# Fused attention and mixture-of-experts on one core: the gate's transposes move ahead of the score projection, its logits move beside the output projection

## What is computed

```python
def _layernorm(x, axis=-1, eps=1e-05): ...
# attention, 8 sequences of 1024 tokens, width 256, the heads not split
qkv = jnp.einsum('bse,he->bsh', x, w_qkv)
q, k, v = jnp.split(qkv, 3, axis=-1)
scores = jnp.einsum('bqh,bkh->bqk', q, k) * scale
out = jnp.einsum('bqk,bkh->bqh', jax.nn.softmax(scores, axis=-1), v)
out = jnp.swapaxes(out, 1, 2).reshape(Bn, Sn, H)
out = jnp.einsum('bsh,eh->bse', out, w_proj) + b_proj
# expert layer: 16 experts, each takes its 1024 best tokens
logits = flat_x @ gate_w.T
scores = jax.nn.softmax(logits, axis=-1).T
topk_weight, topk_idx = jax.lax.top_k(scores, C)
g, u = xg @ Wg.T, xg @ Wu.T                # per expert
h = jax.nn.gelu(g, approximate=False) * u  # then Wd, weighted, scatter-added
# plus a shared expert of the same shape over all tokens
x = x + _layernorm(attention(_layernorm(x)))
x = x + _layernorm(ffn(_layernorm(x)))
```

## Time and profile before

| | us |
|---|---|
| median of three runs | 2094.87 |
| their range | 2094.38 to 2095.66 |
| the profiled execution, its own time | 2094.38 |
| its span in the trace | 2092.6 |
| PE busy | 2019.6 (97%) |
| DVE busy | 1248.5 (60%) |
| ACT busy | 966.9 (46%) |
| POOL busy | 509.3 (24%) |
| granted PE clock, mean, as a share of full speed | 0.985 |

### The profile page before, as it was taken

The page is one execution under the profiler, slowest core; times in us unless marked ns, Lnnn a source line. Parts: engine busy times, 40 slices in busy tenths (PEclk is TensorE's granted clock), DMA queues, the critical chain, the costliest instruction groups (busy, mean ns, idle before and its releaser), DMA issues.

```text
span 2092.6 us, 30112 instructions
## 1 busy us (share of the span) xinstructions
PE 2019.6 (97%) x11290; PEld 1727.2 (83%) x11290; DVE 1248.5 (60%) x2467; ACT 966.9 (46%) x1802; POOL 509.3 (24%) x619
## 2 busy tenths in 40 slices
PE   7999999999994999999999999999999999999996
PEld 6888888888884888888888888888888888888885
DVE  6676676676663877565556556545454545454565
ACT  4564564574542444444434343434344434444443
POOL 0022022022021000224222422332224222432265
PEclk9999999999995999999999999999999999999998
DMA  3011111111015111233333333333333333334266
GB/s 114 1 41 42 61 62 62 40 61 61 36 47 196 69 60 42 99 87 65 90 62 77 75 75 78 76 80 75 81 84 71 92 62 92 75 80 101 54 200 130
DMA packets 55612, 159.77 MB, mean 76 GB/s; under 512 B 9536, under 2 KB 26048, under 8 KB 48320
## 3 DMA queue, kind: packets, MB, share of 16 engines
q1 hardware_dynamic: 28976, 116.16, 15.2%
q0 software_dynamic: 26512, 41.96, 12.5%
HBM read 98.78 MB, written 59.31 MB: 76 GB/s over the span
## 4 chain that ended last, share of the span: by engine, by line
PE 64%; DVE 2%; POOL 1%; ACT 1%; issue 0%; DVEq 0%; another core or an unknown queue 0%; ACTq 0%; POOLq 0%
PE mo_psD L1297 11%; PE mo_psG L58 7%; PE mo_psU L58 7%; PE mo_psU L60 7%; PE mo_psG L60 7%; PE mo_psG L59 7%; PE mo_psU L59 7%; PE mo_psD L1299 6%; PE mo_psX L1223 1%; PE mo_psD L58 1%; PE mo_psD L59 1%; PE mo_psD L60 1%; PE mo_psX L1038 1%; DVE mo_HF L1556 0%; DVE mo_st L1520 0%
## 5 line engine op out<-in xcount | busy, mean ns | idle before, releaser
L1556 DVE TENSOR_TENSOR mo_HF<-mo_psU,mo_HF 128x512 f32<-128x512 f32 x320 | 221.1, 691 | 360.1 <-ACT mo_HF L1396 336.7
L1396 ACT ACTIVATE mo_HF<-mo_psG 128x512 f32<-128x512 f32 x320 | 191.5, 598 | 483.3 <-PE mo_psU L60 407.9
L1791 POOL DMA_INDIRECT ACC<-mo_OUT,mo_GI x128 | 202.9, 1585 | 675.5 <-DVE mo_OUT L1633 666.6
L1297 PE MATMUL mo_psD<-mo_wd,mo_H_hi 128*128 128x512 f32 x1024 | 362.7, 398 | 0.0
L1299 PE MATMUL mo_psD<-mo_wd,mo_H_lo 128*128 128x256 f32 x1024 | 287.5, 281 | 0.0
L1297 PEld LDWEIGHTS mo_psD<-mo_wd,mo_H_hi 128*128 128x128 f32 x1024 | 192.4, 188 | 47.6
L1501 DVE TENSOR_TENSOR mo_H_lo<-mo_HF,mo_H_hi 128x512 fp32r<-128x512 f32 x300 | 204.8, 683 | 0.0
L1374 ACT ACTIVATE mo_H_hi<-mo_HF 128x512 fp32r<-128x512 f32 x320 | 199.5, 623 | 1.1 <-DVE mo_HF L1556 1.1
L1299 PEld LDWEIGHTS mo_psD<-mo_wd,mo_H_lo 128*128 128x128 f32 x1024 | 193.4, 189 | 1.2
L1633 DVE SCALAR_TENSOR_TENSOR mo_OUT<-mo_psD,mo_TW,mo_OUT 128x256 f32<-128x256 f32 x128 | 61.9, 483 | 217.0 <-ACT mo_OUT L1463 214.6
L1463 ACT ACTIVATE mo_OUT<-mo_psD,mo_TW 128x256 f32<-128x256 f32 x128 | 60.9, 476 | 270.1 <-PE mo_psD L1299 195.0
(11 more groups left out here) (260 smaller groups left out, 4963.0 us busy)
## 6 DMA issues: line engine op xcount, KB each, us to landing
X1a<-wg_in SPq DMA_DIRECT2D x16, 1024.0 KB
X1a<-wu_in SPq DMA_DIRECT2D x16, 1024.0 KB, 4.8
X1a<-wd_in SPq DMA_DIRECT2D x16, 1024.0 KB, 4.8
XN<-XNB SPq DMA_DIRECT2D x8, 1088.0 KB, 4.0
X<-x_in SPq DMA_DIRECT2D x8, 1024.0 KB, 6.0
out_dram<-X SPq DMA_DIRECT2D x8, 1024.0 KB, 4.3
XN2T<-xn2T SPq DMA_DIRECT2D x8, 1024.0 KB, 3.8
mo_F<-ACC SPq DMA_DIRECT2D x7, 1024.0 KB, 14.0
```

Of the source, the lines that this page charges most:

```text
L1297: pe.matmul(psD[:, t % 2, :], h_hi, wd_both[:, it, :, :].rearrange("p z d -> p (z d)"), start=(it == 0), stop=False)
L1396: a.activation(HF[:, it % 2, :], psG[:, it % 2, :], ACT.Gelu).then_inc(s_gelu, 1)
L1556: v.tensor_tensor(HF[:, it % 2, :], psU[:, it % 2, :], HF[:, it % 2, :], ALU.mult).then_inc(s_mul, 1)
L1791: g.indirect_dma_start(out=io["ACC"], out_offset=bass.IndirectOffsetOnAxis(ap=GI[n % 2][:, 4 * tb + t:4 * tb + t + 1], axis=0), in_=OUT[:, ...
```

## The change

On PE, the 16 transposes of the `gate` part move from behind T to the head of the round, ahead of T. In bank k they now wait for `xnT_lo` of bank k in place of `tT_lo` of bank k. T waits once for all four `xnT_lo`, in every round, and in rounds with a `gate` part T's bank k also waits for the copy `xn2T` of bank k. Y waits for `tT_lo` in place of `xn2T`. The logits of tiles 2k and 2k+1 follow Y's bank k, where they followed V's bank k. On ACT, the four copies to `xn2T` come ahead of the four `tT_hi`. Rounds 8 and 9 keep their order.

```diff
             def body(R):
                 r = R.r
+                if R.gate:
+                    for k in range(4):
+                        dk, ht = k % 2, k // 2
+                        wait(pe, s_xn2, 2 * (r - 2) + ht + 1 if R.attn else 2 * (r - 1))
+                        if R.attn:
+                            wait(pe, s_xl, 4 * r + k + 1)
+                        for j in range(4):
+                            i = pe.transpose(psS[:, k, j * P:(j + 1) * P], XNB[:, 4 * ht + j, dk * P:(dk + 1) * P], c.ident[:, :])
+                        i.then_inc(s_tr2, 1)
...
                 if R.attn:
+                    wait(pe, s_xl, 4 * (r + 1))
                     for k in range(4):
                         m, h = k % 2, k // 2
-                        wait(pe, s_xl, 4 * r + 2 * h + 2)
+                        if R.gate:
+                            wait(pe, s_n2, 4 * (r - 2) + k + 1)
...
                         i.then_inc(s_tt, 1)
-                if R.gate:
-                    for k in range(4):
...
-                            wait(pe, s_tl, 4 * r + k + 1)
...
                 if R.post:
                     wait(pe, s_ol, 8 * r)
...
-                        if R.gate:
+                        if R.attn:
+                            wait(pe, s_tl, 4 * r + k + 1)
+                        elif R.gate:
                             wait(pe, s_n2, 4 * (r - 2) + k + 1)
-                        elif R.attn:
-                            wait(pe, s_tl, 4 * r + k + 1)
...
                         i.then_inc(s_y, 1)
+                        if R.gate and R.attn:
+                            logits((2 * k, 2 * k + 1))
...
                         i.then_inc(s_v, 1)
-                        if R.gate:
-                            logits((2 * k, 2 * k + 1))
```

More of the change, by code:

```diff
@@ L303, in body @@
                         i.then_inc(s_tt, 1)
-                if R.gate:
-                    for k in range(4):
-                        dk, ht = k % 2, k // 2
-                        wait(pe, s_xn2, 2 * (r - 2) + ht + 1 if R.attn else 2 * (r - 1))
-                        if R.attn:
-                            wait(pe, s_tl, 4 * r + k + 1)
-                        for j in range(4):
-                            i = pe.transpose(psS[:, k, j * P:(j + 1) * P], XNB[:, 4 * ht + j, dk * P:(dk + 1) * P], c.ident[:, :])
-                        i.then_inc(s_tr2, 1)
                 if R.post:
@@ L438, in body @@
                 r = R.r
[L439 to L443, removed]
                 if R.gate:
@@ L451, in body @@
                 if R.attn:
+                    for k in range(4):
+                        m, h = k % 2, k // 2
+                        wait(a, s_tt, 4 * r + k + 1)
+                        a.activation(tT[0][:, m, h * 512:(h + 1) * 512], psS[:, k, :], ACT.Copy).then_inc(s_th, 1)
                     for k in range(4):
```

## The result

| | before | with the change |
|---|---|---|
| median of five runs, us | 2094.38 | 2104.54 |
| their range, us | 2093.34 to 2095.66 | 2103.77 to 2107.85 |
| ratio, 95% interval | | 1.0052 (1.0037 to 1.0066) |
| the profiled execution, us | 2094.38 | 2098.71 |
| its span, us | 2092.6 | 2096.9 |

The kernel is slower by 10.2 us in the medians, where 10.1 was forecast. The profiled execution of the changed kernel is 5.8 us faster than the median of the others, so its trace can't be read by its total. Read by stages it shows two things: the attention block ends 10.8 us later than before, and the expert layer is 6.4 us shorter than before.

A forecast was written before the change was run, and what follows sets the result against it. PE's stream, busy 97% of the span, was taken to set the attention block's end and all that follows. 6.6 + 1.94 + 1.54 = 10.1 us on 2094.38 gave 2104.5 us, range 2101.5 to 2108.5.

The forecast's parts named there:

- The copies ahead of T: Rounds 2 to 7: T waits for ACT's first `xn2T` copy behind the last `O_hi`; 1.1 us a round, 6.6 us.
- waits that ACT must pass: Between `O_hi` and the first copy on ACT: allowance that puts a round's upper end at 1.5 us instead of 1.1.
- The full wait in rounds 0 and 1: T waits for all four `xnT_lo` with no transposes ahead: 1.94 us in round 0, 1.54 us in round 1.
- What bounds the block: Attention block: PE's stream sets its end; PE's largest group of waits is 3.6 us for `PT_lo`.
- Logits beside Y, Y behind `tT_lo`: In the rounds: moving the logits from V to Y and Y's wait from `xn2T` to `tT_lo` costs nothing.
- The clock in round 0: Round 0's long PE idle may halve the clock again: 1.7 us lost, total 2106.2, a bit less likely than not.
- The rivals: Includes the clock falling to half in each of rounds 2 to 7: 10 us more, 2116 with round 0; chance 0.05.
- The rule that the prediction weighed: Rounds 2 to 7: by it each round has over 3 us without counted work; time as the every-round clock rival's, 2116.
- The gap between the blocks: PE's 11.0 us idle before the expert layer swallows the 10.1 us, giving 2093 to 2094.4; chance 0.02.
- the cost would show only in rounds 0 and 1: ACT's copy comes before T needs it in rounds 2 to 7; only 3.5 us left, 2097.9 or 2096.7; chance 0.05.

The follow-up runs named there:

- late_ohi: Changed kernel with T waiting only for the half it reads and ACT's last `O_hi` behind the next round's `xn2T` copies (rounds 2 to 7): 2088.94 against 2091.09, ratio 0.9990.
- copy_twice: Changed kernel with ACT's first copy to `xn2T` made twice, a drain between, in rounds 2 to 7: 2106.91 us against 2091.09 before, ratio 1.0078.
- half_wait: Changed kernel with T waiting only for the half of `xnT_lo` that it reads: 2095.11 us, ratio 1.0040 to the kernel before.
- logits_alone: Kernel before with only the logits moved from beside V to beside Y: 2087.99 us, ratio 1.0001 to the kernel before.

## Why the prediction was right

**The copies ahead of T: 1.1 us a round, 6.6 us.** Measured 1.16 a round from the stores, 7.0 for six. The size is right to 0.06, and the mechanism is shown from both sides: `late_ohi` takes the wait away and gives 1.28 a round back, `copy_twice` makes it longer and costs 0.85. One thing came out otherwise. I took the seam between the starts of `O_hi` and of the next ACT instruction, 0.42 us, from rounds 2 and 7. In loop rounds 4 to 6 of the changed kernel it is longer: ACT's copies start at 319.60, 397.45 and 475.29, each 0.56 or 0.57 us after the start of their `O_hi`, so there Y starts 8.82 to 8.85 us after the head instead of 8.71. The old trace doesn't show this: in its loop rounds the same seam, to `tT_hi`, is 0.42 to 0.44 us, so it is not the loop alone, and why it grew is open. From store to store, the two rounds without this seam got 1.03 and 1.09 us longer, as forecast (1.06 and 1.08), and the three with it 1.22 to 1.24. The range had room for waits that ACT must pass; the longer seam costs 0.15 us in each of three rounds.

**The full wait in rounds 0 and 1: 1.94 and 1.54 us.** In round 0 T starts at 21.22, 1.79 later than before; in round 1 PE waits 1.20 us. `half_wait` against the changed kernel gives 3.8 us in the medians, and the store of round 2 is 3.3 us apart in their traces (192.22 and 195.53 in the same job). The term stands. In the pairs with `late_ohi` the medians show 2.1 and 2.7 us more than the waits, which no step of the prediction explains.

**What bounds the block: right where it counted, read too widely.** The prediction called 3.6 us for `PT_lo` the largest group of PE's waits in the whole attention block. The same view has larger ones at the block's two ends:

```profile
PE psS L311 <- ACT XNB L405: 18.1, 1, 18.1
PE psS L127 <- DMA X1a<-wk_in: 7.3, 1, 7.3
```

Both were there with the change as well (18.1 and 7.1 us), so the forecast lost nothing by it, but PE's stream sets the pace of the rounds only, not of the drain.

**Logits beside Y, Y behind `tT_lo`: nothing.** Both hold: `logits_alone` is at 1.0001, and no wait ahead of Y or V appears.

**The clock in round 0: here the prediction's argument was wrong.** It tied a fall of the clock to the long wait. In the changed kernel T did run slowly in round 0. In its second trace T and then V start at

```profile
21.31 0.76 PE L58 MATMUL psS<-xnT_hi,m 128*128 128x512 f32 x1 [3.37 <-DVE xnT_lo L527]
...
22.72 0.63 PE L58 MATMUL psS<-xnT_hi,m 128*128 128x512 f32 x1
...
28.28 0.28 PE L58 MATMUL psS<-wv,xnT_hi 128*128 128x256 f32 x1
```

6.97 us for T, against 5.54, at a granted clock that went to its lower level:

```profile
22.00:23.00 1.00, 1.00 (x4) 0.50 0.00 0
```

But `logits_alone`, with the old short wait, has the same:

```profile
19.37 0.76 PE L58 MATMUL psS<-xnT_hi,m 128*128 128x512 f32 x1 [1.21 <-DVE xnT_lo L526]
...
20.78 0.63 PE L58 MATMUL psS<-xnT_hi,m 128*128 128x512 f32 x1
...
26.82 0.28 PE L58 MATMUL psS<-wv,xnT_hi 128*128 128x256 f32 x1
```

Of eleven traces, ten have T at 6.97 to 7.63 us in round 0: six after the long wait and four after the short one. The trace of before, at 5.54, is the exception. Until T starts in round 0, `logits_alone` is the kernel before, instruction for instruction. So 1.4 to 2.1 us of loss to the half clock stand in nearly every trace, after either wait, and no trace shows that the change adds them. Why the one trace escaped is open. I had read a single lucky execution as the rule. It had no effect on the predicted time, since it was kept out of the sum, but it spoiled two of my expectations, each by about 2 us.

**The rivals.** In rounds 2 to 7 T never ran at the lower clock after the transposes and 1.0 us of waiting: T takes 5.5 us there (170.46 - 164.91 in round 2). The rule that the prediction weighed, in the Trainium skill ("TensorE: Matmul & The Clock Gate", Part 4: PE-mode transpose), is that transposes don't count as activity for the clock in the way of matmuls; read as the prediction read it, T would have run at the lower clock here. With these float32 transposes it did not: in rounds 3 to 6 of the changed kernel T takes 5.6 us each. The gap between the blocks took nothing up: it is 11.0 us long in both traces and moved with the block. That the cost would show only in rounds 0 and 1 was refuted by the six waits.

**Luck in the total.** The forecast of 2104.5 and the median of 2104.54 agree better than the method deserves. In the first of the later jobs the same change cost 12.2 us, while the terms as the traces give them, 7.0 and 3.3 us, make 10.3; the other 2 us have no known cause. The block's end, 10.77 us later in the first pair of traces, is also less clean than it looks. Up to the store of round 7 the changed kernel is 12.22 us behind (584.90 against 572.68), of which 2.07 are the half clock in T of round 0 (7.61 us against 5.54), so 10.15 are left for the change. From there on the logits of the drain met the lower clock for another length of time in each trace: 1.00 us is added up to the next store and 2.45 are taken off up to the last. The 10.15 us are the forecast's sum; that the block's end is so near to it is chance.

## What to carry to other kernels

Where a step is moved ahead in one engine's stream, look up what the engine that serves it has still to do at that moment: here the transposes could start at once, but their first reader stood behind an unrelated instruction, and the step behind them lost 1.2 us a round on the engine that bounds the kernel. Move the reader together with what it reads. And merging finer waits into one at the front of a step is free only where something covers it: it cost nothing behind the transposes, 1.4 us a round without them.

## What the runs showed that was not expected

- The same instructions of the expert layer ran at two paces. From its first load to the end of the execution it took 1430.5 us in the trace of before, 1424.1 with the change, 1422.3 to 1424.5 in the four traces of the first later job, and 1426.4 to 1429.0 in the five of the other two. In the trace of before an expert's 402 matmuls take 71.6 us and PE is idle for 0.2 us in them; in the first of the changed kernel 70.86 us with no idle time. The granted clock is 1.00 in both. The kernel before itself had medians from 2086.7 to 2094.4 us in four measurements. The cause was not looked for.
- The clock's level in the records is not always there. In the first trace of the changed kernel the row for 22 to 23 us says 1.00, while the matmuls in it start 0.43 us apart, as they do at the lower level elsewhere. In six of the eleven traces the rows say 1.00 all the way from 10 to 31 us, though T's first matmuls stand as far apart in them. The distance of matmuls of one shape is the safer sign.
- The last 32 logits records of the block take 7.01 us in the trace of before and 4.56 in the first of the changed kernel: in the one the granted clock stays at 0.50 throughout them, in the other it is at 1.00 from about 661 to 664. That alone moved the block's end by 2.4 us between executions, and it is a quarter of what was to be measured.
